# Expert rows through memory: a gather in place of a one-hot combine, nine weight places, and a bfloat16 one-hot

## The reference

```python
x = x + tanh(g_xattn[0]) * conv_mixer(ctx, ctx, layernorm(x))      # 16 heads, convolution along 256
x = x + tanh(g_ffn[0])   * moe(layernorm(x))                        # routed and shared experts
x = x + tanh(g_xattn[1]) * attention(layernorm(x), ctx, ctx)        # 16 heads, rotary, 256 x 256 scores
x = x + tanh(g_ffn[1])   * lowrank_moe(layernorm(x))                # 8 experts, top 2

def moe(x):                      # 1024 tokens, 32 experts, top 6, capacity 48 a batch, inter 176
    probs = softmax(group_limited(x @ gate_w.T)); w, e = top_k(probs, 6); w *= 16
    slot = e * 48 + position_of_the_token_within_expert(e)          # dropped past 48
    rows = scatter(x, slot)
    y = (silu(rows @ w_gate) * (rows @ w_up)) @ w_down
    return sum_k w[:, k] * y[slot[:, k]] + shared_expert(x)
```

## Time and profile before

| | |
|---|---|
| median of 3 runs | 492.98 us (491.26 to 493.21) |
| the profiled execution | 491.66 us, of which the span of the trace is 489.8 us |
| TensorE busy | 413.6 us, 84% of the span, 2821 matmuls |
| VectorE | 295.0 us, 60% |
| ACT | 166.6 us, 34% |
| GpSimd | 153.8 us, 31% |
| moved by DMA | 43.5 MB, mean 89 GB/s |
| mean granted clock | 0.927 |

### The profile page before, as it was taken

How to read it: one execution, slowest core, us unless ns; L and a number is a source line. 1 busy time by engine, 2 the same in 40 slices (tenths; PEclk the granted TensorE clock), 3 DMA queues, 4 the chain that set the end, 5 groups by cost and what they waited for, 6 DMA issues and landing times.

```text
span 489.8 us, 7462 instructions
## 1 busy us (share of the span) xinstructions
PE 413.6 (84%) x2821; PEld 266.0 (54%) x2821; DVE 295.0 (60%) x613; ACT 166.6 (34%) x300; POOL 153.8 (31%) x234
## 2 busy tenths in 40 slices
PE   1489993869769768699998768999999989899996
PEld 1378883824535435368886534455555545465554
DVE  1859997499916454633447778688898823322212
ACT  1221320133345434200110125467767785311110
POOL 0658898248972210502111060022112231110000
PEclk9999996588859998999999869699999999899999
DMA  6692010200049999741183141543345000000101
GB/s 197 190 286 87 33 34 32 87 0 0 1 121 267 254 258 233 188 143 36 58 162 83 57 97 34 119 87 75 64 78 98 3 3 1 1 0 1 43 0 43
DMA packets 49867, 43.53 MB, mean 89 GB/s; under 512 B 4101, under 2 KB 48553, under 8 KB 49833
## 3 DMA queue, kind: packets, MB, share of 16 engines
q1 hardware_dynamic: 47264, 40.65, 32.8%
q0 software_dynamic: 800, 2.10, 1.5%
q10 hardware_dynamic: 1768, 0.33, 0.4%
HBM read 36.55 MB, written 6.32 MB: 88 GB/s over the span
## 4 chain that ended last, share of the span: by engine, by line
PE 50%; DMA 16%; POOL 13%; DVE 11%; issue 3%; SPq 3%; ACT 3%; DVEq 0%; POOLq 0%; ACTq 0%
DMA WG<-in_L_ffn_w_gate_up_dram 10%; PE PS L1038 8%; PE PS L1221 7%; PE PS L1184 6%; PE PS L1080 5%; PE PS L1007 5%; PE PS L1065 4%; PE PS L957 3%; DMA R<-qparts_d 3%; DMA X<-in_x_dram 2%; DVE MX L1457 2%; PE PS L1033 2%; POOL SA L430 2%; POOL R L491 2%; SPq L343 2%
## 5 line engine op out<-in xcount | busy, mean ns | idle before, releaser
L1457 DVE TENSOR_REDUCE MX<-PS 128x2 f32<-128x512 f32 x128 | 85.9, 709 | 18.4 <-PE PS L1007 18.0
L708 ACT ACTIVATE R<-PS 128x1024 f32<-128x1024 f32 x64 | 65.4, 1024 | 46.9 <-PE PS L1065 46.5
L1038 PE MATMUL PS<-R 128*128 128x256 bf16 x384 | 47.3, 276 | 0.0
L1007 PE MATMUL PS<-R 72*128 72x256 bf16 x192 | 39.9, 295 | 6.6 <-DVE MX L1457 5.5
L1080 PE MATMUL PS<-R 128*32 128x256 f32 x512 | 42.6, 407 | 1.4 <-ACT R L718 1.0
L1038 PEld LDWEIGHTS PS<-R 128*128 128x128 bf16 x384 | 37.9, 99 | 5.9
L411 POOL TENSOR_TENSOR RSB<-RSA,MH 128x2 f32<-128x2 f32 (+2 forms) x20 | 14.3, 713 | 75.9 <-issue 40.2
L553 POOL TENSOR_TENSOR X<-X,R 128x256 f32<-128x256 f32 x8 | 5.8, 727 | 99.9 <-ACT R L731 99.9
L957 PE MATMUL PS<-WG,R 128*64 128x352 f32 x128 | 24.0, 496 | 14.8 <-DMA WG<-in_L_ffn_w_gate_up_dram 14.2
L1221 PE MATMUL PS<-WG,R 128*128 128x256 f32 x128 | 33.1, 405 | 1.3 <-DVE R L1624 1.2
L1065 PE MATMUL PS<-R 75*128 75x256 bf16 x192 | 31.6, 290 | 1.7 <-DMA R<-MR 1.7
(11 more groups left out here) (237 smaller groups left out, 796.2 us busy)
## 6 DMA issues: line engine op xcount, KB each, us to landing
WG<-in_L_ffn_w_gate_up_dram SPq DMA_DIRECT2D x16, 704.0 KB, 12.6
WD<-in_L_ffn_w_down_dram SPq DMA_DIRECT2D x16, 352.0 KB
R<-kparts_d SPq DMA_DIRECT2D x24, 192.0 KB
R<-qparts_d SPq DMA_DIRECT2D x18, 192.0 KB
R<-kpad_d SPq DMA_DIRECT2D x1, 2048.0 KB, 7.9
kparts_d<-SA SPq DMA_DIRECT2D x4, 384.0 KB, 2.5
qparts_d<-WD SPq DMA_DIRECT2D x4, 384.0 KB, 3.2
SA<-qparts_d SPq DMA_DIRECT2D x6, 192.0 KB
```

The costliest lines, as they stand in the source:

```text
L708: act.activation(PX[:, G % 4].rearrange("p h m n -> p (h m n)"), PS[:, 2 * (G % 2):2 * (G % 2) + 2, :].rearrange("p a n -> p (a n)"), ACT. ...
L1007: last = pe.matmul(PS[:, 4 + H % 2, m * L:m * L + L], QST[b % NST][0:NT, h, m * P:m * P + P], KST[b % NST][0:NT, h, :], start=True, stop=True)
L1038: last = pe.matmul(o, OHT[:, k, b * P:b * P + P], Y[:, k, s, :], start=False, stop=(k == KT0 - 1 and s == 2))
L1457: dve.tensor_reduce(MX[:, H % NH, :], PS[:, 4 + H % 2, :].rearrange("p (m n) -> p m n", m=LB), AX, ALU.max).then_inc(s_max, 1)
```

## The change

- **Combine.** Each pair's output rows, times WS and tanh(g_ffn[0]), are written in float32 to a table `yrows_d` in memory, 2048 rows and a row of zeros. VectorE works out, for each token and each rank r = 0 to 5, the row's number (`slots`, `address`, in the loop). After the loop GpSimd reads six rows per token and batch by indirect DMA (`collect`, 48 reads in all). For batches 0 to 3 TensorE adds the six with an identity matrix in PSUM (`gathered`); for 4 to 7 GpSimd adds them to x (`added`) during attention. The turn of OH, its copies and the three parts of Y are gone.
- **Weights.** Nine places instead of three: three in R1, where OH was, three in R2. OH moves to R2. The pairs 3 to 5 are loaded after the first three, 6 to 8 when the indices are done.
- **One-hot.** OH, its counter and the places are bfloat16, laid out with the pair as the last dimension; a pair's weights for the index matmuls are then 32 bytes apart.
- **Shared expert.** GpSimd's two products become two on VectorE, ACT's four operations become one; the last four `shared` move after the indices and into the loop. `down` runs two pairs behind `up`, not one.
- **Queries.** Five chunks (batches 0; 1; 2 and 3; 4 and 5; 6 and 7) instead of four. `normed` takes the power on GpSimd and the rest of the root on VectorE. Chunks 3 and 4 come in attention, in batches 0 and 1, and 2 and 3.
- **Order.** The roots of the second norm stand ahead of GpSimd's constants. Blocks of ones in the key stacks move to VectorE. SyncE reads stacks of keys and queries apart (`kstack`, `qstack`), and loads the last layer's WA and WB in attention.

```diff
+NPL = 9
+CHUNKS = ((0, 1), (1, 2), (2, 4), (4, 6), (6, 8))
-        IOT = sb("IOT", [P, CAP], F32)
+        IOT = sb("IOT", [P, CAP, KT0], BF16)
-        OH = R1[:, :].bitcast(BF16).rearrange("p (b e c) -> p b e c", b=B, e=E0)
+        OH = r2(0, 8192).bitcast(BF16).rearrange("p (b f c k) -> p b f c k", b=B, f=2, c=SLOTC)
+        PLACE = [(WG[:, 2 * i:2 * i + 2, :, :], WD[:, 2 * i:2 * i + 2, :, :]) for i in range(NPAIR)] \
+            + [pair_place(R1[:, 896 + PAIRW * i:896 + PAIRW * i + PAIRW]) for i in range(3)] \
+            + [pair_place(r2(PAIRW * i, PAIRW)) for i in range(3)]
...
+            for k in range(NPAIR, 2 * NPAIR):
+                load_up(k)
+                load_down(k)
...
+            sp.wait_ge(ix_pe, 1)
+            for k in range(2 * NPAIR, NPL):
+                load_up(k)
+                load_down(k)
+            for k in range(NPL, KT0 + 1):
                 if k < KT0:
-                    sp.wait_ge(gu_pe, k - NPAIR + 1)
+                    sp.wait_ge(gu_pe, k - NPL + 1)
...
+            kstack(0)
+            kstack(1)
+            qout(0)
+            qstack(0)
+            kstack(2)
+            qout(1)
+            qstack(1)
+            kstack(3)
+            maxrow(0)
+            qout(2)
+            qstack(2)
+            qstack(3)
+            maxrow(1)
+            kstack(4)
+            qout(3)
+            maxrow(2)
+            qstack(4)
...
+            for c in range(QC):
+                root(2 * c, 2 * c + 2)
+            pool.wait_ge(conv_done, NH)
+            pool.wait_ge(z_done, NH)
+            pool.memset(OH[:, :, :, CAP:SLOTC, :].rearrange("p b f c k -> p (b f) (c k)"), 0.0).then_inc(const_ok, 1)
...
+            def collect(b, ranks=range(NC)):
+                if b >= 4:
+                    pool.wait_ge(sd_pe, 1)
+                if b >= 6:
+                    pool.wait_ge(mo_pe, 2)
+                for r in ranks:
+                    pool.indirect_dma_start(CBUF[b][:, r, :], None, yrows_d.ap(),
+                                            bass.IndirectOffsetOnAxis(ap=GX[:, b, r:r + 1], axis=0))\
+                        .then_inc(row_in[b][r // 3] if b < 4 else rows_in[b - 4], 16)
+            def added(b):
+                pool.wait_ge(rows_in[b - 4], 16 * NC)
+                pool.wait_ge(mo_x, 2)
+                for r in range(NC):
+                    ins = pool.tensor_tensor(X[:, b, :], X[:, b, :], CBUF[b][:, r, :], ALU.add)
...
+            collect(0)
+            collect(1, range(2))
+            power(0)
+            collect(1, range(2, NC))
+            collect(2, range(2))
+            power(1)
+            collect(2, range(2, NC))
+            collect(3)
+            collect(4)
+            power(2)
+            collect(5)
+            added(4)
+            added(5)
+            pool.wait_ge(added_ok, 2)
+            power(3)
+            collect(6)
+            collect(7)
...
+            def ywrite(k):
+                act.wait_ge(y_ok, k + 1)
+                act.dma_start(yrows_d.ap()[1 + k * P:1 + k * P + P, :], YS[:, k % NYS, :]).then_inc(y_out[k % NYS], 16)
...
-                                     OH[:, b, 2 * k:2 * k + 2, :].rearrange("p e c -> p (e c)"),
+                                     OH[:, b, :, :, k].rearrange("p f c -> p (f c)"),
...
+            def gathered(b):
+                for r in range(NC):
+                    pe.wait_ge(row_in[b][r // 3], 16 * 3)
+                    last = pe.matmul(half[b], IDF[:, :], CBUF[b][:, r, :], start=False, stop=True,
+                                     skip_group_check=True)
+                last.then_inc(mo_pe, 1)
...
+            gathered(0)
+            qproject(0)
+            gathered(1)
+            qproject(1)
+            for H in range(EARLY):
+                smax(H)
+                if H == 7:
+                    gathered(2)
+                if H == 12:
+                    gathered(3)
...
+            ones(0)
+            ones(1)
+            dve.wait_ge(sd_pe, 1)
+            update(4, 6)
+            update(6, 8)
+            for i in range(NYS):
+                dve.wait_ge(y_out[i], 16 * (KT0 // NYS))
+            ones(2)
+            ones(3)
+            for i in range(2):
+                dve.wait_ge(mo_pe, i + 1)
+                update(i, i + 1)
+                normed(i)
+                qterm(i, 0)
+                qterm(i, 1)
+                qsum(i)
+                qrest(i)
+                qlow(i)
+            for H in range(EARLY):
+                rowmax(H)
+                if H == 13:
+                    dve.wait_ge(mo_pe, 4)
+                    update(2, 4)
+                    normed(2)
...
```

More of the change, by code:

```diff
@@ new lines, in _ @@
+            pool.wait_ge(v32_ok, 2)
+            done(pool.memset(SELE[:, :, :], 0.0))
+            for s in range(3):
+                done(pool.affine_select(out=SELE[:, :, :], in_=SELE[:, :, :], compare_op=ALU.not_equal,
+                                        fill=1.0, base=-s * E1, pattern=[[-1, E1], [0, P]],
+                                        channel_multiplier=1))
+            def collect(b, ranks=range(NC)):
[7 more added lines that the diff above has]
+                        .then_inc(row_in[b][r // 3] if b < 4 else rows_in[b - 4], 16)
@@ L556, in _ @@
                 root(b, b + 1)
+                if b == 0:
+                    added(6)
+                    added(7)
+                    pool.wait_ge(added_ok, 4)
+                    power(4)
                 if b == B - 3:
@@ L633, in _ @@
                 for s in range(2):
-                    cast(KR["parts"], KR["a"], c, s, False)
+                    cast(c, s)
                     if s == 0:
@@ L693, in _, with qcast @@
                     xbcopy(k + 1)
-                if k + 2 < KT0:
-                    ohcopy(k + 2)
+                if k >= 3:
+                    ywrite(k - 3)
             atcopy(KT0 - 1)
-            for c in range(QC - 1):
+            for k in range(KT0 - 3, KT0):
+                ywrite(k)
+            def qcast(i, s):
+                n = (CHUNKS[i][1] - CHUNKS[i][0]) * L
+                if i >= 1 and s == 0:
+                    act.wait_ge(qp_out[i - 1], 32)
+                act.wait_ge(cast_in, 2 * i + s + 1)
+                act.activation(QR["parts"][:, s, 0:n], QR["a"][:, 0:n], ACT.Copy).then_inc(cast_out, 1)
+            for i in range(2):
                 for s in range(2):
-                    cast(QR["parts"], QR["a"], c, s, True)
+                    qcast(i, s)
+            qcast(2, 0)
             sc = 1.0 / float(HD) ** 0.5
@@ L919, in _ @@
             last.then_inc(pos_pe, 1)
-            for u in range(2, 6):
-                shared(u)
+            shared(2)
             pe.wait_ge(rh_ok, 1)
@@ L986, in _ @@
                 up(k)
+                if k < 2:
+                    shared(4 + k)
                 if k >= 1:
@@ L1415, in _, with slots, address, addresses @@
                 rows = slice(eo * 64, eo * 64 + 64)
-                done(dve.tensor_reduce(WS[rows, :],
-                                       ixv[rows, :, 2 + eo:8][:, :, 0:5:2], AX, ALU.add))
+                done(dve.tensor_reduce(WS[rows, :], ixv[rows, :, 2 + eo:8][:, :, 0:5:2], AX, ALU.add))
+            for u in range(1, 4):
+                shared(u)
+            def slots():
+                v = VL.rearrange("p (b e) -> p b e", b=B)
+                done(dve.tensor_tensor(v, v, bc(EIO[:, :], sh3, 1), ALU.mult))
+                done(dve.tensor_tensor(ADR, ADR, VL, ALU.add))
+            def address(r):
+                tmp = GTM[:, r % 2, :].rearrange("p (b e) -> p b e", b=B)
+                done(dve.scalar_tensor_tensor(out=tmp, in0=PF, scalar=float(r + 1),
+                                              in1=ADR.rearrange("p (b e) -> p b e", b=B),
+                                              op0=ALU.is_equal, op1=ALU.mult))
+                done(dve.tensor_reduce(GF[:, :, r], tmp, AX, ALU.add))
+            def addresses():
+                dve.tensor_copy(GX[:, :, :], GF[:, :, :]).then_inc(gx_ok, 1)
             def silu(k):
@@ new lines, in _, with update @@
+            ones(0)
+            ones(1)
+            def update(b0, b1):
+                v = X[:, b0:b1, :].rearrange("p b l -> p (b l)")
+                o = PS[:, b0 // 2, (b0 % 2) * L:(b0 % 2) * L + (b1 - b0) * L]
+                ins = dve.tensor_tensor(v, v, o, ALU.add)
+                ins.then_inc(mo_x, 1)
+                n_x[0] += 1
+                dve.wait_ge(mo_x, n_x[0])
+            n_x = [0]
+            dve.wait_ge(sd_pe, 1)
+            update(4, 6)
+            update(6, 8)
@@ L1505, in normal @@
+            qsum(2)
             def normal(b, m):
```

571 lines of the change are left out of this document (293 added, 278 removed).

## The result

The changed kernel takes **533.79 us** (median; 531.35 to 545.33), the kernel before beside it 492.12. The ratio is 1.085 (95% interval 1.074 to 1.096): 8.5% slower, where 470 us was forecast. The profiled execution took 533.22 us, its span is 531.4. The time of one and the same kernel moves with the granted clock from execution to execution, so medians are given with their spread and ratios leave disturbed runs out; the profiles of e1 (529.29 us), e3 (528.86), e14 (510.17) and e16 (491.75) are of such longer executions.

What follows compares the result with a forecast made beforehand. The prediction took the expert loop to be bound by weight DMA, the combine by TensorE. From the 489.8 us span: -29.6 to loop end, +0.3 to first exponential, +7 attention, giving 467.5 span, 470 us in all; range 451 to 486.

Steps and rivals of the forecast that it cites:

- signs of being wrong: Loop still ending past 195, GpSimd's reads over 2.4 us apart, or attention growing by over 15 us.
- Part 1: Before the expert loop: first up projection at 127 instead of 139.7 us.
- (b): Before the loop: `shared` leaves GpSimd, so VectorE shares nothing there; -2.8 us to the compares.
- (c): One-hot compares: bfloat16 operands with step one take about 0.96 us each, with 1.76 as upper end.
- (a): Second norm: square roots no longer stand behind GpSimd's constants; 1.2 us come back.
- (d): First indirect read leaves at once, not 2.2 us after the indices; `shared(3)`, 3.5 us, runs beside its 2.7 us flight.
- "nothing" for the early loads: Three more weight pairs read from 31 to 45 us, when only K's parts need a queue, cost nothing.
- Part 2: Expert loop: DMA stays the bound, barely; loop end 183.3 instead of 212.9, -29.6 us including the earlier start.
- Part 3: Loop end to first exponential: a chain through GpSimd, VectorE and DMAs takes 69.6 us against 69.3, no gain.
- Part 4: Attention: late query chunks cost +4.5, +4 and +0.5, less 2 in batch 0; rounded to +7 us.
- "-2" in my sum: Attention, batch 0: loses late projection and blocks of ones, but batch 2's Q reaches memory only after its third step; -2 us.
- The slower one: Rival: between loop and first row maxima, indirect reads of freshly written rows go one after another at 2.9 us; 503 us, chance 0.09.

Runs made afterwards that it cites:

- e1: Changed kernel without the 24 indirect reads of batches 4 to 7 and GpSimd's 24 additions; 525.81 us, ratio 1.069.
- e3: Changed kernel with the last layer's weights read after the sixth batch's maxima instead of before the last stacks; 524.79 us, ratio 1.074.
- e14: e12 with the products of the two late chunks one step later and batch 5's reads behind the third write of queries; 502.26 us, ratio 1.029.
- e16: Kernel before the change with only the bfloat16 one-hot in the new layout, pair as innermost dimension; 491.46 us, ratio 1.000.
- e5: Changed kernel with weights of pairs 3 to 5 loaded after the writes of K's parts, and GpSimd's padding fill after the last norm; one execution, 532.76 us.
- e6: Changed kernel with weights of pairs 6 to 8 read only after the first gathered rows have been turned; 526.46 us.
- e2: Changed kernel with the second query chunk written before the third key stack is read, and batch 4's reads after the third chunk's power; 529.78 us.
- e4: Changed kernel with the maxima's rows written by ACT's queue after each batch's sixth exponential, instead of by SyncE; 537.15 us, ratio 1.102.
- e12: Changed kernel with e2 to e7 together, first maxima before the third chunk's cut, that chunk finished before the first exponential, key stacks 2 and 3 later; 508.98 us.
- e10: Changed kernel with 26 unused float32 products of constants added on TensorE just ahead of waits for transfers; 520.04 us, ratio 1.068.
- e15: e14 with nine unused products of constants added on TensorE ahead of waits; 501.9 us, ratio 1.029.
- e7: Changed kernel with VectorE's four blocks of ones written as 2048 float32 words each, all ahead of the wait for the shared expert's products; 528.56 us.

## Why the prediction was wrong

By its own steps, against the profiled execution; the misses add up to 63.9 us, span 531.4 against 467.5. Of the prediction's own signs of being wrong one came: attention grew by 43 us, not by under 15. Three of its additions are slightly off (28.7 us and not 28.9, 70.2 and not 69.6, 470.7 and not 470), which changes nothing.

- **Part 1: -12.7 forecast, -2.2 found.** (b) and (c) were right: from the logits' copy to the compares 13.95 us instead of 16.66, 2.7 saved of 2.8; a compare 0.952; from compares to indices 11.75 against 12.35. *(a) failed*, for what was put in its place: the memset that fills the padding now runs beside the last norm, whose two operations take 4.08 us together instead of 0.73 (e5). I had listed the order and not asked what VectorE does beside the fill. The Trainium skill (SBUF — State Buffer, "Who interferes with whom") says that a VectorE `tensor_scalar` in a two-port mode and a GpSimd instruction exclude each other for the whole instruction; by that rule the trace agrees in length: 4.08 is 3.51 of memset and the rest. That these operations run in such a mode no row shows. *(d) failed*: I put nothing beside the first read, though the diff issues 3.2 MB of weights at the same event; it landed in 7.8 us, and `shared(3)` ran mostly at the lower clock level (granted 0.57), 6.15 us for 3.5; e6 shows that without the loads this second cost alone keeps the up projection back. And *"nothing" for the early loads failed*: the first write of K's parts stood behind them, 9.84 us for 2.5, and the last heads came 3.8 us later; in e5, with the loads behind the writes, they end at 77.3, as before the change (77.5).
- **Part 2: right in sum, wrong in cause.** From first up projection to loop end 55.8 us against 56.3. But it was never bound by DMA: the 2.67 us a pair that I had worked out for TensorE is 2.77, and ran to the end. The loop ended 10 us late only because it began so.
- **Part 3: 69.6 forecast, 83.7 found.** The chain held as far as the first write: first power at +22.1, the write at +29.4 (forecast 28.9), memsets 4.28 us apart as priced. The second chunk's write then left at +43.3, behind a stack in SyncE's order. *Its landing* failed: priced like any other (2.2 to 2.5), it took 23.2 us behind 0.6 MB of stack and beside indirect reads of some 1.6 MB. I had asked of the reads only how they delay each other, not who shares the DMA engines with them. e1 (landing 13.3, first exponential 10.4 us earlier after the loop) and e2 (under 5.6, 5.1 earlier) show it.
- **Part 4: +7 forecast, +43 found**, the step with the largest error. I priced the work that came in, the two chunks (4.5 and 4; found 3.7 and 4.9 above a usual step), and no transfer of SyncE's. The third chunk's write inside batch 0 (gap 9.9; "-2" in my sum), the maxima of batch 2 behind `qout(3)` (7.4) and those of batch 5 behind 2.1 MB of weights and two stacks (11.8; "late, but 30 us before use", which looked at the weights and not at the queue behind them) are 22 us of gaps above usual steps. e3, e4, e12 and e14 show what each stood behind, and that behind one gap the next transfer waited. And the sum knew nothing of the clock: 20.6 us of attention and 3.5 of the last layer are nearly the same products at a lower granted clock. That waits bring this level about is shown only in part: e10 got 4.0 us back in batch 2 and nothing in batches 0 and 5.
- **The rivals.** None gave a time near 534. The slower one named the right engine and the wrong victim: the reads were not late themselves (1.26 us apart, as priced) but kept the DMA engines from the write. Its 503 had no price for others. How much of the clock's part would go with the waits could not be separated further: e15's products lifted the clock and met VectorE's chunk instead.
- With transfers and order mended (e14) the ratio goes from 1.085 to 1.029: two thirds of the loss come back. The last third stays open; in e15 the mean granted clock is 0.866 against 0.927 of the kernel before. No version here beats the kernel before.

## What to carry to other kernels

Before pricing a transfer, list what is issued within 20 us ahead of it on every queue, and for SyncE what stands between it and the last wait; a write that was 2.5 us in a quiet stretch can be 23. The combine that kept TensorE busy (65.4 of 69.3 us) ran at a granted clock of 0.98, the stretch in its place (46.9 of 83.7 us) at 0.67, and attention behind it at 0.77 instead of 0.92: where work is taken off TensorE and waits take its place, put a slower case at the lower level beside the sum (here up to 26.2 against 14.6 us a batch). Before an early load is called free, ask which transfer is due behind it. And when a wait is removed, ask which one is next: in e3 and e4 a gap of 6 us came up inside batch 4 when that ahead of batch 5 went.

## What the runs showed of the hardware

- Indirect reads of 128 rows of 1 KB cost the DMA engines more beside other transfers. Alone (214 to 222.7 us) four of them took 22.0% of all sixteen, 1.91 us, 0.48 us each, and landed in 2.8 us. In the 23.2 us above, beside SyncE's transfers, 1.58 MB took 63.8%, 14.8 us, 1.23 us for each read of 0.131 MB: at 1.26 us from issue to issue that nearly fills the engines. SyncE's transfers cost about the same in both cases: 0.165 x 23.2 / 0.82 = 4.7 us a MB there, 4.9 with stacks alone (333.7 to 349 us: 1.77 MB, 56.4%). Why the reads cost 2.6 times as much is not shown.
- SyncE's issues grow too: 2.87 us for one that takes 0.39 in a quiet stretch.
- VectorE memsets in a row start 1.04 ns an element apart, in bfloat16 (4096 elements: 4.28 us) and in float32 (2048: 2.14), for a value other than zero as well; the rows give only 3.47 and 1.76 of it as duration. The Trainium skill (VectorE: DVE Perf Modes, "Zero memsets can be issued as uint32") says one cycle an element whatever the type, which at the 0.96 GHz of the same page is an estimate of 1.04 ns; by that rule the trace agrees. Of the 8.6 us that e7 saved on VectorE 3 reached the first power.
- TensorE's weights (128 x 128, bfloat16) with a step of 32 bytes take 159 ns a load in the changed kernel (median, granted clock 0.50) and 166 in e16 (0.79), against 97 for weights side by side in the kernel before.
